# The edge MLP of a graph network: two steps per transpose and per product, and narrow closings of the sums

## The reference, cut to what matters

```python
# layer 2: edge MLP
e = jnp.concatenate([h[row], h[col]], axis=1)      # 100000 x 256
e = jax.nn.silu(e @ We1 + be1)                      # 100000 x 64
e = jax.nn.silu(e @ We2 + be2)                      # 100000 x 64
agg = jax.ops.segment_sum(e, row, num_segments=6250)
out = jax.nn.silu(jnp.concatenate([h, agg], axis=1) @ Wn1 + bn1) @ Wn2 + bn2
# layer 3: twice
out = segment_sum((x @ W)[row] * norm[:, None], col, num_segments=n) + b
```

## Time and profile before

| | |
|---|---|
| median of 3 runs | 5980.8 us (5976.45 to 5984.49) |
| the profiled execution | 5983.38 us |
| its span, first to last instruction | 5981.4 us |
| mean granted clock of TensorE | 0.628 |
| PE busy | 3703.9 us (62%) |
| PE's weight loads busy (PEld) | 3022.9 us (51%) |
| DVE busy | 3076.2 us (51%) |
| ACT busy | 1681.4 us (28%) |
| POOL busy | 4075.3 us (68%) |

### The profile page before, as it was taken

How to read it: one execution, slowest core, us unless ns; L and a number is a source line. 1 busy time by engine, 2 the same in 40 slices (tenths; PEclk the granted TensorE clock), 3 DMA queues, 4 the chain that set the end, 5 groups by cost and what they waited for, 6 DMA issues and landing times. The chain is left out here.

```text
span 5981.4 us, 90476 instructions
## 1 busy us (share of the span) xinstructions
PE 3703.9 (62%) x20158; PEld 3022.9 (51%) x20159; DVE 3076.2 (51%) x10705; ACT 1681.4 (28%) x5852; POOL 4075.3 (68%) x4183
## 2 busy tenths in 40 slices
PE   4344444356777777679999999545445455455452
PEld 2333333345666666568888887333333343333332
DVE  5787777666777777643333333533333343333336
ACT  2333333336777777422222222100000000000000
POOL 2677777756777777357777771477777747777773
PEclk7555555567877777865555556765665665656656
DMA  3111112212333333111111210111111111111111
GB/s 98 51 52 52 52 52 56 48 49 86 104 104 104 104 104 104 48 48 52 52 51 51 55 51 12 46 53 52 52 52 52 52 48 53 52 52 52 52 52 39
DMA packets 210751, 358.53 MB, mean 60 GB/s; under 512 B 87268, under 2 KB 123698, under 8 KB 210502
## 3 DMA queue, kind: packets, MB, share of 16 engines
q0 software_dynamic: 142944, 296.35, 18.2%
q1 hardware_dynamic: 67558, 59.16, 3.2%
HBM read 332.22 MB, written 26.33 MB: 60 GB/s over the span
## 5 line engine op out<-in xcount | busy, mean ns | idle before, releaser
L2027 POOL DMA_INDIRECT arena<-table_gcn,idx_now x1568 | 1499.9, 957 | 487.9 <-issue 417.8
L2074 PE MATMUL pair<-arena,hotf 128*128 x3328 | 752.4, 418 | 996.2 <-DMA arena<-table_gcn,idx_now 995.6
L2074 PEld LDWEIGHTS pair<-arena,hotf 128*128 128x128 f32 x3328 | 702.3, 321 | 1129.9 <-issue 1129.7
L540 POOL DMA_INDIRECT arena<-table_attention,idx_now x832 | 827.7, 995 | 276.6 <-issue 186.9
L540 POOL DMA_INDIRECT arena<-table_key_value,idx_now x832 | 796.2, 957 | 258.9 <-issue 220.5
L1676 POOL DMA_INDIRECT arena<-table_edge_mlp,idx_now x784 | 782.1, 998 | 243.2 <-issue 214.9
L2101 DVE TENSOR_TENSOR acc<-acc,pair 128x1024 f32 x208 | 253.9, 1221 | 1348.0 <-PE pair L2077 1347.6
L998 PE MATMUL pair<-wide,hotf 128*128 128x130 f32 x1664 | 428.1, 437 | 644.7 <-ACT wide L962 644.7
L998 PEld LDWEIGHTS pair<-wide,hotf 128*128 128x128 f32 x1664 | 366.4, 324 | 708.8 <-ACT wide L962 708.8
L2036 ACT COPY idx_now<-src_t 128x8 int32 (+1 forms) x204 | 39.3, 197 | 1885.0 <-PE pair L2077 1875.3
L2091 DVE TENSOR_SCALAR hotf<-iota,rel_now,ew_now 128x128 f32<-128x128 f32 x1664 | 454.6, 360 | 7.7 <-ACT ew_now L2041 7.7
(11 more groups left out here) (350 smaller groups left out, 6983.7 us busy)
## 6 DMA issues: line engine op xcount, KB each, us to landing
arena<-rel_dram SPq DMA_DIRECT2D x52, 512.0 KB
arena<-table_gcn,idx_now POOLq DMA_INDIRECT x1568, 2.5
arena<-table_attention,idx_now POOLq DMA_INDIRECT x832
arena<-table_key_value,idx_now POOLq DMA_INDIRECT x832
arena<-table_edge_mlp,idx_now POOLq DMA_INDIRECT x784, 2.4
table_key_value<-arena SPq DMA_DIRECT2D x13, 512.0 KB, 2.9
table_gcn<-tab SPq DMA_DIRECT2D x26, 256.0 KB, 2.3
table_attention<-arena SPq DMA_DIRECT2D x13, 264.0 KB, 2.5
```

The source lines that it names most:

```text
L540: q_.indirect_dma_start(ring[:, slot, 0:width], None, table, bass.IndirectOffsetOnAxis(ap=idx_now[:, slot:slot + 1].bitcast(U32), axis=0)) ...
L2027: q_.indirect_dma_start(conv_ring[:, slot * D:(slot + 1) * D], None, table, bass.IndirectOffsetOnAxis(ap=idx_now[:, slot:slot + 1].bitcast ...
L2074: t_.matmul(window[:, bass.ds(offset * D, D)], hot8[:, g % 2, u, :], conv_ring[:, bass.ds(slot * D, D)], start=False, stop=False)
```

## The change

In the edge MLP two neighbouring steps are turned by one transpose of 128 x 128 (2 x 64 features) in place of two of 128 x 64, and multiplied by one product whose moving side is a 128 x 128 matrix with `We2` twice on its diagonal. So `turn` has 4 transposes and `second_product` 4 products of 128 columns. The bias, which no longer fits in as a 65th row, is now written by a product ahead of them that opens the bank: 3 rows of ones against 3 rows of bf16 parts of the bias (`ones3`, `bias2`, 512 columns); it stands ahead of the wait for `l2_s1T_kept`. ACT copies 128 x 512 in place of 64 x 1024. The three bias rows are made by DVE at the end of the block before, and two corners of `we2` are cleared in the first block. The closing products of zeros are 2 columns wide in place of 512, in the edge MLP (one for each group) and in both convolutions (two for each group).

```diff
-        we2 = sb("we2", [EH + 1, EH])
+        we2 = sb("we2", [P, P])
+        be2b = sb("be2b", [P, EH])
...
-                    w(we2[0:EH, :], We2)
-                    w(we2[EH:EH + 1, :], be2.rearrange("(one o) -> one o", one=1))
+                    w(we2[0:EH, 0:EH], We2)
+                    w(we2[EH:P, EH:P], We2)
+                    row(be2b[:, :], be2)
...
+                ch(v.memset(we2[0:EH, EH:P], 0.0))
+                ch(v.memset(we2[EH:P, 0:EH], 0.0))
...
                 v.memset(zeros2, 0.0)
+                ch = Chain(dve, n2_bias)
+                ch(v.memset(ones3, 1.0))
+                ch(v.tensor_copy(be2_b[:, 0, :], be2b[:, :]))
...
+                ch(v.tensor_copy(bias2.rearrange("p (u f) -> p u f", u=CG), be2p[0:3, 3, :].unsqueeze(1).to_broadcast([3, CG, EH])))
                 dve.wait_ge(n2_rows, 32)
-                v.memset(s1T[EH:EH + 1, :, :], 1.0)
...
-        LB, ST, EB = bank[0:2], pair[1], bank[4]
+        LB, ST, EB = bank[0:2], bank[2], bank[4]
...
-                    s_.copy(s1T[0:EH, g % 2, :], ST[0:EH, :]).then_inc(l2_s1T_kept, 1)
+                    s_.copy(s1T[:, g % 2, :], ST).then_inc(l2_s1T_kept, 1)
...
-                    for u in range(CG):
-                        last = t_.transpose(ST[0:EH, u * P:(u + 1) * P], junk[:, g % 2, u * EH:(u + 1) * EH], ident[:, :])
+                    for u in range(CG // 2):
+                        at = slice(u * P, (u + 1) * P)
+                        last = t_.transpose(ST[:, at], junk[:, g % 2, at], ident[:, :])
                     last.then_inc(l2_s1T, 1)
 
                 def second_product(k, g):
+                    at_least(pe, l2_s2, k, 0)
+                    t_.matmul(EB, ones3, bias2, start=True, stop=False)
                     pe.wait_ge(l2_s1T_kept, k + 1)
-                    at_least(pe, l2_s2, k, 0)
-                    for u in range(CG):
-                        last = t_.matmul(EB[:, u * EH:(u + 1) * EH], s1T[:, g % 2, u * P:(u + 1) * P], we2[:, :], start=True, stop=True)
+                    for u in range(CG // 2):
+                        at = slice(u * P, (u + 1) * P)
+                        last = t_.matmul(EB[:, at], s1T[:, g % 2, at], we2[:, :], start=False, stop=(u == CG // 2 - 1))
                     last.then_inc(l2_e, 1)
...
-                    t_.matmul(window, zeros2[:, 0:P], zeros2, start=False, stop=True).then_inc(l2_sum, 1)
+                    t_.matmul(window[:, 0:2], zeros2[:, 0:P], zeros2[:, 0:2], start=False, stop=True).then_inc(l2_sum, 1)
...
                         for h in range(2):
-                            last = t_.matmul(window[:, h * 512:(h + 1) * 512], zeros[:, 0:P], zeros, start=False, stop=True)
+                            last = t_.matmul(window[:, h * 512:h * 512 + 2], zeros[:, 0:P], zeros[:, 0:2], start=False, stop=True)
```

More of the change, by code:

```diff
@@ L238, in tab_rows @@
             return tabf[0:rows, at[0] - words:at[0]]
-        s1T = tab_rows(2 * CG * P, EH + 1).rearrange("p (k c) -> p k c", k=2)
+        s1T = tab_rows(CG * P).rearrange("p (k c) -> p k c", k=2)
+        bias2 = tab_rows(CG * EH // 2, 3).bitcast(BF16)
+        ones3 = tab_rows(P // 2, 3).bitcast(BF16)
         step2_slot, step2_offset, step2_node = (tab_rows(STEPS, 1).bitcast(I32) for _ in range(3))
@@ L253, in build @@
         sort_b = hotT[:, :, :].rearrange("p a b -> p (a b)").bitcast(F32)
+        be2p = junk[:, 0, 0:4 * EH].rearrange("p (c f) -> p c f", c=4)
+        be2_b = junk[:, 1, 0:3 * EH // 2].bitcast(BF16).rearrange("p (c f) -> p c f", c=3)
+        is_row = junk[:, 1, P:P + 3]
         pre_now = hot[:, :, :, :].rearrange("p a b c -> p (a b c)").bitcast(F32).rearrange("p (k u f) -> p k u f", k=2, u=CG)
@@ L1442, in build @@
              "e_mm", "e_kept", "e0", "e_rest", "e1", "split", "t2_out", "t2_free", "copied", "vector", "factor"))
-        n2_rows = sem("n2_rows")
+        n2_rows, n2_bias = sem("n2_rows"), sem("n2_bias")
         N2 = 1 + NORM
@@ L1511, in _ @@
                 v.memset(zeros2, 0.0)
+                ch = Chain(dve, n2_bias)
+                ch(v.memset(ones3, 1.0))
+                ch(v.tensor_copy(be2_b[:, 0, :], be2b[:, :]))
+                for c in range(3):
+                    ch(v.tensor_scalar(out=is_row[:, c:c + 1], in0=part[:, 0:1], scalar1=float(c), scalar2=None, op0=ALU.is_equal))
+                ch.wait()
+                for c in (1, 2):
+                    ch(v.tensor_sub(be2p[:, c, :], be2p[:, c - 1, :] if c > 1 else be2b[:, :], be2_b[:, c - 1, :]))
+                    ch.wait()
+                    ch(v.tensor_copy(be2_b[:, c, :], be2p[:, c, :]))
+                    ch.wait()
+                ch(v.tensor_scalar(out=be2p[:, 3, :], in0=be2_b[:, 0, :], scalar1=is_row[:, 0:1], scalar2=None, op0=ALU.mult))
+                for c in (1, 2):
+                    ch.wait()
+                    ch(v.scalar_tensor_tensor(out=be2p[:, 3, :], in0=be2_b[:, c, :], scalar=is_row[:, c:c + 1], in1=be2p[:, 3, :],
+                                              op0=ALU.mult, op1=ALU.add))
+                ch.wait()
+                ch(v.tensor_copy(bias2.rearrange("p (u f) -> p u f", u=CG), be2p[0:3, 3, :].unsqueeze(1).to_broadcast([3, CG, EH])))
                 dve.wait_ge(n2_rows, 32)
-                v.memset(s1T[EH:EH + 1, :, :], 1.0)
                 by_group = step2_node[:, 0:STEPS].rearrange("p (k u) -> p k u", u=CG)
```

## The result

The changed kernel took 5950.1 us (median of 5 runs, 5946.5 to 5961.9) against 5980.8 us of the kernel before (5 runs on the same chip), 31 us faster by the medians where 53.5 were forecast. The ratio on record is 0.9956, 95% interval 0.9945 to 0.9967, which is 26 us (20 to 33); the quotient of the two medians, 0.9949, lies inside the interval. On a second chip the ratio was 0.9966 (0.9954 to 0.9978). The profiled executions took 5983.4 before and 5948.3 after, 35.1 us apart.

What follows compares the result with a forecast made beforehand. POOL's fetch pace was taken to bound the edge MLP up to the last fetch, PE the tail. Savings 27.4 + 1 + 5.0 + 19.0 - 1.3 + 2.4 = 53.5 us, from 5980.8 to 5927; range 5902 to 5960.

Steps and rivals of the forecast that it cites:

- What bounds the kernel: Edge MLP: POOL's fetch pace, 10.05 us per 8 fetches, sets when rows arrive; PE alone bounds after the last fetch.
- Term 1: POOL's fetches in the edge MLP: with PE ahead, their stretch falls from 33.4 to 6 us, saving 27.4.
- third rival: Edge MLP: L1816 starts just ahead of a fetch in each of 98 groups, costing 100 us; 6021 us, chance 0.06.
- Term 2: Start of the edge MLP's tail: rows after the last fetch come 1 us sooner and PE's lateness of 5.0 us goes.
- Term 3: Edge MLP's tail after the last fetch: cheaper turns, second products and closings save 19.0 us at the present clock mix.
- Term 4: Block before the edge MLP: thirteen small operations making the bias rows replace L1513, costing 1.3 us.
- Term 5: Both convolutions: narrow closings save 1.2 us at the end of each, 2.4 in all.
- wide passes: Edge MLP's second product: passes cost by their moving columns, 0.44 us each; about 5971 us, chance 0.05.
- The clock: Edge MLP's tail: PE's clock rises to 2.4 GHz for some 6 groups, another 19 us saved; 5908 us, chance 0.14.
- The phase's loss: Edge MLP: L1816 starting ahead of a fetch costs that fetch 1.02 us, in each of 98 groups; chance 0.06.
- the signs: Expected in the profile after: among others, PE idle about 1.3 us in each edge MLP group, ended by ACT's silu.
- Only PE's own time: Edge MLP: POOL's stretch stays at 33.4 us and only PE's work shrinks, saving 26 us; 5955 us, chance 0.17.

## Why the prediction was wrong

The direction was right and the gain was half of the forecast: 31 us by the medians, 26 by the ratio, 35 in the profiles, for 53.5. Term by term the profiles give 16.0 for 27.4, 5.2 for 6.0, 13.1 for 19.0 and 1.1 for 2.4; the stretch up to the first fetch gave 2.0 where 1.3 was to be lost, and 2.2 went in the block between, which no term spoke of.

**What bounds the kernel: this step failed as an explanation.** "POOL's own pace sets when rows arrive" is true, and it does not set the end of the stage. PE, busy 893 of 900 us in the earlier trace rows, did, at the mix of clocks that it was granted: 104 groups of PE from 2605.4 to 3706.0 are 10.58 us each, above POOL's 10.41 (1019.8 / 98; 10.05 and the stretch). "PE is full but, over the stage, not late by more than the six groups" only says that the ring of rows hides the lateness until the tail. Taking the stretch away alone gave 0, not 27. The stages tell it: 1114.5 before, 1111.8 with POOL unstretched, 1111.1 with narrow closings, 1110.1 with pairs and three more openings, all with PE full. In the six profiles in which a group of PE at 1.2 GHz (9.15, or 9.55 with wide closings) is below POOL's 10.05 they are 1067 to 1086, and 1078 to 1080 in the three of the changed kernel. So the pairs are the cause of the gain; the smaller stretch is how part of it becomes visible. How little a smaller cut of PE's work brings is the other half: 0.43 us a group brought 3.4 us in the stage and no gain in time, because the clock fell with it. The prediction took the mix of clocks as given.

**Term 1, mis-sized: 16.0 for 27.4.** With PE ahead, the stretch is 17.3, 12.2 and 11.7 us in three profiles of the changed kernel, not 6. The 0.03 of a group came from 32 quiet groups, in which DVE was idle, had no gap, and started 2.54 to 2.71 us after the group's last fetch. The sentence "When DVE stands idle for the rows, L1810 starts 2.54 to 2.71 us after" holds only for these. Of the 68 waits before, 23 ended more than 3 us after the last fetch, with 9.3 us of stretch: late rows are just what the choice left out. In the trace after, 12 groups have rows that start DVE 3.2 to 4.2 us after the last fetch, and these give 8.3 us; gaps of 0.3 us inside the additions and lags of 2.74 to 2.86 us give 3.0; six groups with a lag of 2.48 to 2.55 give 6.0. The last is the third rival's edge, met in 6 groups instead of 98.

**Term 2, right: 5.2 for 6.0 (1 and 5.0).** The group of the last fetch is turned at 3599.39, 6.13 us after that fetch, where it was 11.34.

**Term 3, mis-sized: 13.1 for 19.0.** The second product has the forecast load time, 8 in 1.78 us, but its stretch of PE is 2.01 with the switch behind it; the turn is 1.02 for 0.85; bias 0.53 and closing 0.11 as forecast. A group at 1.2 GHz is 9.15 for 8.70, saved 1.97 and not 2.42, and 8 groups of this are 3.6 of the 5.9 us that are missing. The rest I put down to the clock, which is argued from the rows and not tried: it is 0.54 over both tails, but of the eight second products from the turn on two ran at 2.4 GHz before, and one after (1.16 us at 3619.09, seven at about 2.0), and in two further profiles of the changed kernel the tail is at 0.50 and 79 us long, which leaves about 10 for this term. "At the mix of clocks of now" was not a safe assumption.

The Trainium skill (TensorE: Matmul & The Clock Gate, "LDWEIGHTS (loading the stationary operand)") gives a load as its columns / 1.2 in ns, which for the 8 loads of the second product would be 8 x 107 = 0.86 us, an estimate. The trace disagrees: 1.78 at 1.2 GHz, as the row of the block before said.

**Term 4, right: 1.27 for 1.3.** From the clearing of `zeros2` to DVE's end were 3.52 us, and are 4.79 (2582.36 to 2587.15). One waited step is 0.25 us (L1528 at 2583.89, L1530 at 2584.15, L1528 at 2584.38), cheaper than the 0.34 assumed, and the four operations ahead of them (2582.60 to 2583.89) were dearer.

**Term 5, not seen: 1.1 for 2.4.** The two convolutions' tails shrink from 30.3 and 32.4 us to 29.6 and 29.5, 3.6 us, and 2.3 of these are lost in the block between the two, which no edit touches. Other profiles say that this is chance: both convolutions together take 2089.5 and 2088.9 us in two more of the changed kernel, 2086.7 and 2083.2 with wide closings, and 2086.6 before. A gain of 2.4 us cannot be told in them. The period of the last groups stays DVE's.

The rivals: wide passes did not cost by their moving columns (1.78, not 3.5). The clock did not rise in the tail of the profiled run (0.54), though it did in one with wide closings (0.65). The phase's loss is real and small. A group of PE was idle for ACT's silu as the signs said, 92.9 us in the stage or 0.9 a group for the 1.3 named. "Only PE's own time" at 5955 came nearest to the measured 5950, but its reason, a stretch that stays at 33.4, did not hold.

## What to carry to other kernels

When one engine paces the arrivals and another is busy 99% of the time, suspect the second, however large the buffer between them: divide the whole stage by its groups and compare with both paces. A stall on the other engine can then be worth nothing until the full one drops below it, as here (25.6 us of stall taken away, 22.9 us longer tail). Work taken off an engine that is full at a mix of clocks need not be worth its time either: price it with the mix that is left, and ask whether it brings the engine below the other's pace even at the low clock. When a rate for the new state is read from a subset of the old one, count what the choice of the subset threw away.

## What the runs showed of the hardware

- A fetch of GpSimd that starts inside a DVE operation ends 0.82 us or a little more behind it, not only for two-input operations. Behind a compare of 128x128 with one tensor input it grows by 0.06 to 0.15 us, behind a bf16 operation of 128x1024 by 0.12 in the mean, 0.32 at most. DVE can pay too: L1828, the bf16 operation, takes 0.48 us alone and 0.68 beside a fetch that started first in the rows at 3600.23 and 3301.23 of the trace after, while L1845 keeps its 1.21 to 1.25 in the 76 groups where a fetch started first. The Trainium skill (SBUF — State Buffer, "SBUF: two separate sides") names an exclusive lock that delays whoever comes second; the trace agrees for the fetches, and for DVE only in the bf16 operation.
- Late rows come at fixed places of a loop unrolled over 12 groups, two of the twelve. In the trace after, all 12 late landings have a packet of the instruction queue between the group's last fetch and the rows, and of the 85 prompt ones 10 have. In the landing shown above that packet has 16 KB. That it is the cause was not tried.
- How much of its time PE is granted 2.4 GHz went with its work per group: 116 us of the stage in the kernel before (11.1 us a group at 1.2 GHz), 82 with narrow closings (10.7), 55 with pairs and four openings (10.4), and 17, 14 and 3 in the three profiles of the changed kernel (9.15). In these profiles less work a group went with less time at the higher clock; by what rule it is granted no run here was made to show.
- On some chips the same kernels ran 22 to 24% longer, with PE idle for "issue" inside groups (284 us of the stage in one run, 7 on the first chip). The versions with the pairs gained 0.9 to 1.5% there and 0.3 to 0.4% elsewhere. What slows PE there stays open.
